# A two-layer transformer block: other waits at the ends of the feed-forward parts, expert rows fetched one part earlier, the second attention layer's first stacks on two queues

## The reference

```python
x = x + attn_a(layernorm(x), ...)
x = x + ffn(layernorm(x), ...)
x = x + attn_b(layernorm(x), Wq, Wk, Wv, Wo)     # 16 heads of 16, causal, rotary
x = x + ffn(layernorm(x), ...)

def ffn(x, ...):
    xln = ln(x); att_out = sigmoid(xln @ Wr) * (xln @ Wv) @ Wo
    x = x + att_out;  h = ln(x)
    winners = argmax(confidences * capital_shares * difficulty + h @ W_aff)   # one of 3 experts
    out_0, out_1 = square(relu(h @ K[e])) @ V[e]                              # e = 0, 1
    out_2 = h @ W1 * sigmoid(state @ W2) @ W3
    return x + out_winner * win_conf / (win_conf + 1e-6)
```

## Time and profile before

| | us |
|---|---|
| median of 3 executions | 2417.39 (2413.64 to 2419.33) |
| profiled execution, its own time | 2412.47 |
| its span | 2410.7 |
| TensorE busy | 2150.9 (89%) |
| VectorE busy | 1486.6 (62%) |
| ScalarE busy | 1027.4 (43%) |
| GpSimd busy | 680.2 (28%) |
| mean granted TensorE clock | 0.95 of full |

### The profile page before, as it was taken

One profiled execution on the slowest core, in us unless ns is written; L12 is line 12 of the kernel. 1 busy time (PEld: TensorE's weight loads), 2 busy tenths in 40 slices (PEclk: granted clock), 3 DMA queues, 4 the chain that ended last, 5 costly groups with the idle time before them and its releaser, 6 DMA issues. The chain is left out here.

```text
span 2410.7 us, 49639 instructions
## 1 busy us (share of the span) xinstructions
PE 2150.9 (89%) x19430; PEld 1743.2 (72%) x19430; DVE 1486.6 (62%) x3884; ACT 1027.4 (43%) x1986; POOL 680.2 (28%) x772
## 2 busy tenths in 40 slices
PE   7799999999999998798789964889999878987998
PEld 7688888888888887677589952445544447766998
DVE  2565664746566474588646645777777628874665
ACT  4343434434343443344245521455555543433554
POOL 3210110201011111266512224433333215662222
PEclk8899999999999999899889987899999989998999
DMA  7300000000000000421657765544455226113775
GB/s 238 119 19 11 10 10 10 19 2 19 10 11 10 10 1 25 110 66 58 241 158 228 236 168 94 90 83 86 84 87 87 43 87 204 42 44 117 231 225 139
DMA packets 155905, 212.84 MB, mean 88 GB/s; under 512 B 51656, under 2 KB 140000, under 8 KB 150368
## 3 DMA queue, kind: packets, MB, share of 16 engines
q1 hardware_dynamic: 142140, 191.51, 27.9%
q0 software_dynamic: 12864, 17.38, 4.4%
q10 hardware_dynamic: 672, 0.79, 0.2%
HBM read 141.93 MB, written 67.69 MB: 87 GB/s over the span
## 5 line engine op out<-in xcount | busy, mean ns | idle before, releaser
L2382 DVE CUSTOM_DVE_ANT_0 bank<-bank,b_raw_masks 128x512 f32<-128x512 f32 (+3 forms) x512 | 239.2, 518 | 140.1 <-PE bank L2609 134.7
L2505 ACT ACTIVATE b_probsT<-bank 128x512 f32<-128x512 f32 x320 | 181.0, 603 | 171.3 <-PE bank L2609 140.1
L2114 PE MATMUL bank<-e_hT_hi,k_rwkv 128*128 128x256 f32 x1088 | 213.0, 282 | 2.8 <-DVE e_hT_lo L2017 2.8
L2114 PEld LDWEIGHTS bank<-e_hT_hi,k_rwkv 128*128 128x128 f32 x1088 | 176.1, 190 | 3.6 <-DVE e_hT_lo L2017 3.6
L2609 PE MATMUL bank<-b_k_stacked,b_q_stacked 96*128 96x512 bf16 (+3 forms) x512 | 127.3, 313 | 54.2 <-DMA b_k_stacked<-scratch_b_parts 26.9
L789 POOL TENSOR_TENSOR probs<-probs,rcp 128x512 f32<-128x512 f32 x64 | 66.9, 1045 | 345.3 <-DVE rcp L658 345.3
L2128 PE MATMUL bank<-v_rwkv_hi,e_hidden_hi 128*128 (+1 forms) x544 | 153.7, 282 | 0.0
L2128 PE MATMUL bank<-v_rwkv_hi,e_hidden_lo 128*128 (+1 forms) x544 | 153.6, 282 | 0.0
L2128 PE MATMUL bank<-v_rwkv_lo,e_hidden_hi 128*128 (+1 forms) x544 | 152.0, 279 | 0.0
L2114 PE MATMUL bank<-e_hT_lo,k_rwkv 128*128 128x256 f32 x544 | 151.5, 279 | 0.0
L2075 ACT ACTIVATE e_relu<-bank,k_bias 128x256 f32<-128x256 f32 x272 | 113.5, 470 | 71.6 <-PE bank L2114 58.0
(11 more groups left out here) (360 smaller groups left out, 6102.7 us busy)
## 6 DMA issues: line engine op xcount, KB each, us to landing
k_rwkv<-scratch_k SPq DMA_DIRECT2D x32, 2048.0 KB, 7.4
scratch_b_parts<-b_part SPq DMA_DIRECT2D x96, 128.0 KB, 1.9
b_q_stacked<-scratch_b_parts SPq DMA_DIRECT2D x96, 128.0 KB, 4.3
b_k_stacked<-scratch_b_parts SPq DMA_DIRECT2D x96, 128.0 KB, 4.4
e_rows<-scratch_rows SPq DMA_DIRECT2D x34, 258.0 KB, 7.6
scratch_rows<-f_hq SPq DMA_DIRECT2D x16, 516.0 KB, 8.4
x_tokens<-in_x_dram SPq DMA_DIRECT2D x8, 512.0 KB, 8.4
scratch_x_out<-x_tokens SPq DMA_DIRECT2D x8, 512.0 KB, 2.9
```

Of the source, the lines that this page charges most:

```text
L2114: last = nc.tensor.matmul(data[:, half * ROWS:(half + 1) * ROWS], ff.k_part(i % 2, a)[:, k, at:at + P], hT[b][:, i % 2, k], start=n == 0, ...
L2382: last = nc.vector.tensor_tensor_reduce(data[:, at:at + size], data[:, at:at + size], raw_masks[:, T - size:T], -1.0, LARGEST, ALU.add, AL ...
L2505: nc.scalar.activation(probsT[:, ring, u], fl.data("st", pair, u)[:], ACT.Exp, scale=DB ** -0.5).then_inc(fl.released("st", pair, u), 1)
```

## The change

1. **Ends of the routing parts.** SP no longer waits for the stored `x`, GpSimd no longer for the scattered rows. SP waits for the scatters itself (`first_rows`) and loads the rows of the first two tiles before it stores the last batch of `x`. For that `f_hq` and `e_rows` become one buffer, `ff.rows`. The wait for the stored `x` stands now on GpSimd ahead of the first add.
2. **Ends of the expert parts.** The wait for the last adds moves from GpSimd to SP. In run 0 SP then issues the load of batch 0 of `x` for `layer_b`, still inside the expert part.
3. **Start of `layer_b`.** SP loads the masks first, then wq, wk, cos, sin, then wv and wo, then batches 1 and 2 of `x`; batches 3 to 7 come behind the first q stack. TensorE's wait for all seven loads and for the constants is split by user. Batch 0 makes its third and fourth `qk` and both `v` in slots -10 and -9 (`FIRST`). `fill_ones` and the load of the rows of ones come earlier. The first k parts are stored and stacked by ScalarE's queue, in the row order 3, 4, 5, 0, 1, 2, beside the first q stack on SP's queue.

```diff
@@ -1108,6 +1109,7 @@
 SQ_RING = AHEAD + 1
+SEQUENCE = [0, TILES - 1, *range(1, TILES - 1)]
@@ -1125,14 +1127,21 @@
 class FeedForward:
-    def __init__(self, nc, ctx, run):
-        self.run = run
+    def __init__(self, core, ctx, run):
+        nc, self.run = core.nc, run
+        self.rows = sbuf(nc, ctx, f"rows_{run}", [P, 2, TT, ROW])
+        self.rows_loaded = [core.signals.sem(f"rows_loaded{p}_{run}") for p in range(2)]
+        self.x_stored = core.signals.sem(f"x_stored_{run}")
...
+    def load_rows(self, eng, moe, i, at):
+        eng.dma_start(self.rows[:, i % 2, 0:RT], moe.rows[at * ROWS:(at + 1) * ROWS, :].rearrange("(t p) c -> p t c", p=P)).then_inc(
+            self.rows_loaded[i % 2], 16)
@@ -1165,7 +1174,7 @@
 xn, xq, x1 = (buf(n, [P, TT, C]) for n in ("f_xn", "f_xq", "f_x1"))
-hq = buf("f_hq", [P, 2, TT, ROW])
+hq, x_stored = ff.rows, ff.x_stored
@@ -1290,6 +1299,16 @@
                  cols(x, n * XB, XB).rearrange("p (t c) -> p t c", c=C)).then_inc(x_stored, 16)
+def first_rows():
+    for n in (B - 2, B - 1):
+        for k in range(CT):
+            sp.wait_ge(*full("hT", n, k))
+    for p in range(2):
+        sp.wait_ge(*scattered(p, B // 2))
+    for i in range(2):
+        ff.load_rows(sp, moe, i, SEQUENCE[i])
@@ -1341,6 +1360,8 @@
 for n in range(6, B):
+    if n == B - 1:
+        first_rows()
@@ -1350,10 +1371,11 @@
     for n in range(B):
+        if n == B - 1:
+            first_rows()
...
     sp.wait_ge(back["v"], 32)
-sp.wait_ge(x_stored, 16 * B)
@@ -1656,8 +1678,6 @@
 scatter(B - 1)
-for p in range(2):
-    ready(scattered(p, B // 2))
@@ -1978,11 +1998,9 @@
 def load_rows(i):
-    if i >= 2:
-        sp.wait_ge(*full("hT", i - 2))
-        sp.wait_ge(s["taken"], (i - 1) * 2)
-    at = sequence[i] * ROWS
-    sp.dma_start(rows[:, i % 2], moe.rows[at:at + ROWS, :].rearrange("(t p) c -> p t c", p=P)).then_inc(rows_loaded[i % 2], 16)
+    sp.wait_ge(*full("hT", i - 2))
+    sp.wait_ge(s["taken"], (i - 1) * 2)
+    ff.load_rows(sp, moe, i, sequence[i])
@@ -1990,14 +2008,17 @@
-load_rows(0)
-load_rows(1)
...
     sp.wait_ge(k_loaded[p], 32 * (of_parity(p) - 1))
+for p in range(2):
+    sp.wait_ge(*added(p, of_parity(p)))
+if run == 0:
+    sp.dma_start(cols(core.x, 0, XB).rearrange("p (t c) -> p t c", c=C),
+                 x_out[0:T, :].rearrange("(t p) c -> p t c", p=P)).then_inc(core.x_first, 16)
@@ -2053,10 +2074,9 @@
+pool.wait_ge(ff.x_stored, 16 * B)
...
     add_rows(i)
-for p in range(2):
-    pool.wait_ge(*added(p, of_parity(p)))
@@ -2160,7 +2180,9 @@
 FIRST_KEYS = (0, 1)
+FIRST_X = 3
 LEAD = 7
+FIRST = {"qk": (-12, -11, -10, -9), "v": (-10, -9)}
@@ -2218,6 +2241,11 @@
     return [(n, i) for i, offset in enumerate(offsets) for n in [batch_at(slot, offset)] if n is not None]
+def inputs_at(slot, kind):
+    first = [(0, i) for i, at in enumerate(FIRST[kind]) if at == slot]
+    return first + [(n, i) for n, i in steps_at(slot, FRONT[kind]) if n]
@@ -2268,6 +2296,12 @@
+def stack(eng, side, b, at, rows=range(len(Q_PARTS))):
+    for row in rows:
+        eng.dma_start(stacked[side][b][row * DB:(row + 1) * DB, :, :],
+                      parts_out[at, (Q_PARTS, K_PARTS_B)[side][row]].rearrange("(h d) t -> d h t", d=DB)).then_inc(stack_loaded[b], 16)
@@ -2286,44 +2320,41 @@
     sp.wait_ge(s["parts_stored"], (at - 1) * 48)
-    for row, c in enumerate((Q_PARTS, K_PARTS_B)[side]):
-        sp.dma_start(stacked[side][b][row * DB:(row + 1) * DB, :, :],
-                     parts_out[at, c].rearrange("(h d) t -> d h t", d=DB)).then_inc(stack_loaded[b], 16)
-load_x(0)
+    stack(sp, side, b, at)
+sp.dma_start(raw_masks[:], dram["masks"]).then_inc(s["masks_loaded"], 16)
+for dst, name in ((wq, "WqT"), (wk, "WkT")):
+    sp.dma_start(dst[:], dram[name].rearrange("(k p) n -> p k n", p=P)).then_inc(s["loaded"], 16)
+for dst, name in ((cos, "cos"), (sin, "sin")):
+    sp.dma_start(dst[:], dram[name]).then_inc(s["loaded"], 16)
+for dst, name in ((wv, "WvT"), (wo, "WoT")):
+    sp.dma_start(dst[:], dram[name].rearrange("(k p) n -> p k n", p=P)).then_inc(s["late_loaded"], 16)
 core.clear_last(sp)
-for dst, name in ((wq, "WqT"), (wk, "WkT"), (wv, "WvT"), (wo, "WoT")):
-    sp.dma_start(dst[:], dram[name].rearrange("(k p) n -> p k n", p=P)).then_inc(s["loaded"], 16)
-for dst, name in ((cos, "cos"), (sin, "sin"), (raw_masks, "masks")):
-    sp.dma_start(dst[:], dram[name]).then_inc(s["loaded"], 16)
-for n in range(1, B):
+for n in range(1, FIRST_X):
     load_x(n)
-sp.wait_ge(s["lo_done"], 1)
-for c in range(3):
-    sp.dma_start(parts_out[0, c], parts[c][:, 0]).then_inc(s["first_stored"], 16)
-sp.wait_ge(s["keys_split"], 1)
-for c in range(3):
-    sp.dma_start(parts_out[1, c], parts[c][:, 1]).then_inc(s["first_stored"], 16)
-sp.wait_ge(s["first_stored"], 96)
-for side in range(2):
-    for row, c in enumerate((Q_PARTS, K_PARTS_B)[side]):
-        sp.dma_start(stacked[side][0][row * DB:(row + 1) * DB, :, :],
-                     parts_out[side, c].rearrange("(h d) t -> d h t", d=DB)).then_inc(stack_loaded[0], 16)
...
                  max_out[B * 2].rearrange("(c h) t -> c h t", h=HEADS_H)).then_inc(s["rows_loaded"], 16)
+sp.wait_ge(s["lo_done"], 1)
+for c in range(3):
+    sp.dma_start(parts_out[0, c], parts[c][:, 0]).then_inc(s["first_stored"], 16)
+sp.wait_ge(s["first_stored"], 48)
+stack(sp, 0, 0, 0)
+for n in range(FIRST_X, B):
+    load_x(n)
...
 sp.wait_ge(s["loaded"], LOADS)
+sp.wait_ge(s["late_loaded"], LATE)
...
 for b in range(STACK_BUFS):
-    sp.wait_ge(stack_loaded[b], B * 2 // STACK_BUFS * 2 * len(Q_PARTS) * 16)
+    sp.wait_ge(stack_loaded[b], B * 2 // STACK_BUFS * STACK_DMAS * 16)
@@ -2408,19 +2439,20 @@
     first_keys()
-    fill_ones()
...
     if u == 2:
-        for n, step in steps_at(slot, FRONT["qk"]):
+        for n, step in inputs_at(slot, "qk"):
...
     normalise(batch_at(slot, FRONT["xn"]))
+if slot == FRONT["xn"]:
+    fill_ones()
@@ -2509,7 +2541,7 @@
 if at in (2, 3):
-    act.wait_ge(s["first_stored"], 96)
+    act.wait_ge(*((s["first_stored"], 48) if at == 2 else (s["keys_stored"], 48)))
@@ -2518,6 +2550,12 @@
 nc.scalar.activation(parts[1][:, at % 2], rotated[:, at % 2], ACT.Copy).then_inc(s["mid_done"], 1)
+if (n, step) == FIRST_KEYS:
+    act.wait_ge(s["keys_split"], 1)
+    for c in range(3):
+        act.dma_start(parts_out[1, c], parts[c][:, 1]).then_inc(s["keys_stored"], 16)
+    act.wait_ge(s["keys_stored"], 48)
+    stack(act, 1, 0, 1, (3, 4, 5, 0, 1, 2))
@@ -2556,7 +2594,7 @@
-act.wait_ge(s["loaded"], LOADS)
+act.wait_ge(s["masks_loaded"], 16)
@@ -2617,6 +2655,8 @@
 if kind in ("qk", "v"):
+    if n == 0:
+        pe.wait_ge(*((s["loaded"], LOADS) if kind == "qk" else (s["late_loaded"], LATE)))
@@ -2670,8 +2710,7 @@
-pe.wait_ge(s["loaded"], LOADS)
-pe.wait_ge(s["consts_done"], CONSTS)
+pe.wait_ge(core.ident_loaded, 16)
@@ -2686,7 +2725,8 @@
 half = half_of(pair)
-pe.wait_ge(stack_loaded[half % STACK_BUFS], 2 * len(Q_PARTS) * 16 * (half // STACK_BUFS + 1))
+pe.wait_ge(s["consts_done"], CONSTS)
+pe.wait_ge(stack_loaded[half % STACK_BUFS], STACK_DMAS * 16 * (half // STACK_BUFS + 1))
```

38 lines of the change are left out of this document (20 added, 18 removed).

## The result

The changed kernel takes 2404.48 us (median of 4 runs, 2402.72 to 2408.2) where the kernel before takes 2418.36 us on the same chip (4 runs, 2413.64 to 2422.64). The ratio is 0.9936, interval [0.9908, 0.9963]: **15.5 us faster, between 8.9 and 22.3**. The forecast was 24.7 us. It is faster, as said, by about three fifths of the sum.

A forecast was written before the change was run, and what follows sets the result against it. TensorE was taken as busy for most of the span, so only seams where all engines stand count. 10.6 + 2.8 + 11.3 = 24.7 us off 2417.39 gave 2392.7 us; own range 2385 to 2399, with two rivals 2381 to 2403.

The forecast's parts named there:

- the seams: Places between stages where all engines stand; each microsecond taken there was said to move all that follows.
- Ends of the routing parts, 10.6 us: Ahead of both expert parts: row loads no longer wait for stored x, TensorE starts 5.3 us earlier in each.
- I take nothing of that: Start of the expert parts: possible higher clock behind a shorter gap, 1.45 us each, left out of the sum.
- End of the expert parts, 2.8 us: Wait for last adds on SP lets GpSimd's drain run beside the transfer; 2.8 us at the program's end.
- Start of the second layer, 11.3 us: From batch 0's load to first turned scores: 11.3 us earlier, including 4.6 up to TensorE and 5.5 at first scores.
- about 2.3 us of k work are left by then, which sharing stretches by 1 us: First stacks: the x loads beside the k stack's end delay first scores from 1463.7 to 1464.7.
- the bound of 7.5 us: First stacks, worst case: x loads fully in between put first scores at 1471.2, a loss of 1.0 us.
- From the first to the first turned scores: Second layer: second half's first scores 10.3 us earlier, limited by its stacks behind x; 1 us more to turned scores.
- Second half late: Rival, chance 0.15: x stands ahead of the second half's stacks, layer gains only 3.3 us; 16.7 us, 2400.7 us.
- Side by side: Rival, chance 0.22: q and k stacks load at once on two queues, first scores at 1459.5; 29.1 us, 2388.3 us.
- The drain stays: Rival, chance 0.05: the 3.2 us belong to the adds, the program's end gives nothing; 20.4 us, 2397.0 us.
- Slower: Rival, chance 0.03: later halves' first scores wait for stacks at 14 boundaries, costing 30.4 us; 2423.1 us.

The follow-up runs named there:

- routing_aligned: routing_alone with 32 unused bytes ahead of the experts' turned rows; 2407.61 us, ratio 0.9948 to the kernel before.
- routing_alone: The kernel before with only the edits at the ends of the routing parts; 2413.18 against 2419.63 us, ratio 0.9973.
- the four others: Four other profiled kernels with the second layer and the wait ahead of it unchanged; first turned scores 96.1 to 97.9 us behind the last add's issue.
- x_behind: The changed kernel with batches 3 to 7 of x loaded behind the stacks of batch 0's second half; 2399.66 us, ratio 0.9918 to the kernel before.
- plain_order: x_behind with the six rows of the first k stack issued in plain order; 2400.51 us, ratio 0.9915 to the kernel before.
- one_queue: x_behind with the first k stack issued on SyncE's queue behind the q stack; 2402.15 us, ratio 0.9915 to the kernel before.
- all_aligned: x_behind with 32 unused bytes ahead of the experts' turned rows; 2393.10 us, ratio 0.9896 to the kernel before.
- layer_alone: The kernel before with only the second layer's edits, first batch of x loaded at the layer's head; 2416.73 us, ratio 0.9985.

## Why the prediction was right or wrong

**The direction and the seams were right.** Small savings at the seams move all that follows: the three parts alone gave 6.5, 4.4 and 3.6 us, together 14.5, and the whole 15.5.

**Ends of the routing parts, 10.6 us.** The seam itself held: 5.1 and 5.0 us between last scatter and first turning, with the rows in time. Two things behind it were not in the sum. First, the term "I take nothing of that" for the clock: it was not 1.45 us per part to win but a small loss. Behind the shorter gap the turning began at the full clock, which fell during it (in run 1 at its very start), and behind the first hidden product it then stayed at 0.50 for 4.9 us instead of 2.9. In the layouts that are free of the address effect the parts are 0.6 us longer than before, 1.3 in all. Second, the row buffers were taken as free because they only changed hands. Moving them cost the other 2.3 us per part, 4.6 in all (206.7 against 204.4 in routing_aligned). No row of before could show that. The trace gives 10.1 - 5.9 = 4.2 us for this part, routing_alone measured 6.5 (3.1 to 9.7).

**End of the expert parts, 2.8 us.** It gave 1.7 at the program's end. The failed step is my own comparison: I set GpSimd's drain, ending "at most" at 1425.4, beside the transfer's landing at 1424.4, and then counted only the landing. With the drain as the later one, 1425.4 + 0.49 = 1425.9, which is 5.3 us behind the issue; the trace has 5.37 and 5.42. The reading of before was right: the DRAIN there takes 2.81 us and starts behind the wait. But with the wait on SP it ended 3.6 us behind the issue's end at both places, later than SP, and became the last.

**Start of the second layer, 11.3 us; it gave 6.3 by the profile of before, 8.7 to 10.4 by the four others.** Up to TensorE 12.4 us was exact, the q stack's issue was 0.2 us off. The k stack's issue was 1.6 us late (33.5 instead of 31.9), for its store was waited for 4.1 us and not 2.68, but that did not matter: 13.1 us from the q stack's issue to the first scores held without `x`: 13.0 in x_behind and plain_order, 12.6 in one_queue, 14.5 in all_aligned. The failed step is "about 2.3 us of k work are left by then, which sharing stretches by 1 us". With so little of k left, the loads of `x`, issued behind the q stack on SP's queue, would move only some 11 us on, about when that stack had landed. But issuing the q stack takes 2.8 us and its loads land 4.0 us behind their issue (median), so `x` was under way when most of k was not, and it shared with k from there. The first scores come 5.4 us later than without it (48.44 against 43.05). That was inside the bound of 7.5 us that I named for `x` fully in between.

**From the first to the first turned scores.** 39.0 us against 38.4 forecast. The second half's stacks, which I had as the limit, were not: SP issued them at 1473.39 behind a store that took 10.4 us to land, and still the second half's scores waited for VectorE and not for them. That 39.0 came so near has some luck in it: the stretch took 44.2 us in the profile of before but 46.2 to 46.8 in the four others, so it fell by more than the 5.8 us of the sum, and at a granted clock of 0.59 against 0.73. *Second half late* did not happen.

**The rivals.** *Side by side* is refuted by one_queue. *The drain stays* came in part: the end gave 1.7 us and not 2.8. *Slower* did not come: layer_alone passes its gain on.

**The range.** By the two traces the 24.7 us lost 0.5 at the routing ends, 5.9 in the expert parts, 1.1 at the program's end and 5.0 in the layer, 12.5 in all, and 12.2 are left; 15.5 were measured, since the layer's start in the profiled execution of before was 2.4 to 4.1 us quicker than in the four others. Each error alone was within its low end, save the address effect, but all fell on the same side. The sum was made against a profiled execution near the fastest of its kernel; runs of the kernel before reach from 2412.86 to 2430.3 us over the sessions. The range was too narrow toward small gains. That all_aligned reached 25.2 us, near the 24.7, does not bear the sum out: its routing parts and the program's end still gave less than forecast, its layer more (12.6 to 14.4 us against the four others).
